# Moving the attention front's pieces to other steps inside the slots stage of a four-layer kernel

## The reference

```
# attention (channel-wise heads, 16 of 8 channels)
q, k, v = x @ qkv_w.T + qkv_b
k = layernorm(k);  v = layernorm(v)                  # over the 8 channels of a head
kv = einsum('bhqd,bhqe->bhde', k, v) / Q * temperature + attn_bias
att = einsum('bhqd,bhde->bhqe', q, kv) + x
out = gelu(att @ p1_w.T + p1_b) @ p2_w.T + p2_b + x
# ffn (soft mixture of experts, 16 experts of 64 slots)
x = layernorm(x) * g + b;  logits = einsum('bnd,esd->bnes', x, layernorm(slot_embeds) * scale)
dispatch = softmax(logits, over tokens);  combine = softmax(logits, over all slots)
slots = einsum('bnd,bnes->besd', x, dispatch)
eout = (gelu(slots @ Wg + bg) * (slots @ Wu + bu)) @ Wd + bd
out = combine @ eout
```

## Time and profile before

| | us |
|---|---|
| median of three runs | 2087.67 |
| the profiled execution's own time | 2088.02 |
| its span, first to last instruction | 2086.20 |
| TensorE busy | 1903.0 (91%) |
| VectorE busy | 1672.0 (80%) |
| ScalarE busy | 1492.8 (72%) |
| GpSimd busy | 1214.2 (58%) |
| granted TensorE clock, mean | 0.963 of full |

### The profile page before, as it was taken

How to read it: one execution, slowest core, us unless ns; L and a number is a source line. 1 busy time by engine, 2 the same in 40 slices (tenths; PEclk the granted TensorE clock), 3 DMA queues, 4 the chain that set the end, 5 groups by cost and what they waited for, 6 DMA issues and landing times.

```text
span 2086.2 us, 38852 instructions
## 1 busy us (share of the span) xinstructions
PE 1903.0 (91%) x13494; PEld 1465.1 (70%) x13494; DVE 1672.0 (80%) x3871; ACT 1492.8 (72%) x2979; POOL 1214.2 (58%) x1026
## 2 busy tenths in 40 slices
PE   4899999999999999688996999999999888889998
PEld 3677676767777676554684888888887666668797
DVE  7898999999998997376197888888888787764686
ACT  5788888888888887254376777777777677776675
POOL 3878888787978875167063555555555544437300
PEclk7999999999999999599997999999999999999999
DMA  6999898898989884201000000000001000012000
GB/s 189 335 308 324 298 319 298 312 308 305 318 302 322 297 300 167 92 1 40 1 7 1 1 1 1 1 1 1 1 1 32 1 1 1 1 38 85 11 1 41
DMA packets 72264, 263.99 MB, mean 127 GB/s; under 512 B 10822, under 2 KB 30406, under 8 KB 71558
## 3 DMA queue, kind: packets, MB, share of 16 engines
q1 hardware_dynamic: 71126, 256.53, 36.1%
q10 hardware_dynamic: 944, 4.98, 0.6%
HBM read 140.17 MB, written 121.31 MB: 125 GB/s over the span
## 4 chain that ended last, share of the span: by engine, by line
PE 42%; DVE 6%; ACT 6%; POOL 1%; issue 1%; DVEq 0%; ACTq 0%; POOLq 0%
PE PS L157 11%; PE PS L335 8%; PE PS L161 8%; PE PS L163 8%; PE PS L162 8%; ACT AR L167 3%; ACT L167 1%; DVE DR L181 1%; DVE AR L185 1%; ACT PT L171 1%; DVE PT L181 1%; POOL AR L176 1%; DVE AR L193 1%; POOL X L181 0%; DVE AR L181 0%
## 5 line engine op out<-in xcount | busy, mean ns | idle before, releaser
L167 ACT ACTIVATE AR<-PS,AR 128x512 f32<-128x512 f32 x1024 | 698.7, 690 | 204.1 <-DVE AR L193 91.3
L193 DVE TENSOR_REDUCE AR<-PS 128x1 f32<-128x512 f32 x896 | 615.4, 687 | 91.8 <-PE PS L163 76.4
L335 PE MATMUL PS<-ident,AR 128*128 128x128 f32 x3816 | 581.7, 277 | 30.6 <-DVE PT L181 16.2
L335 PEld LDWEIGHTS PS<-ident,AR 128*128 128x128 f32 x3816 | 445.2, 142 | 124.9 <-issue 44.2
L157 PE MATMUL PS<-AR 128*128 128x128 bf16 (+7 forms) x4126 | 485.7, 357 | 48.8 <-DVE AR L1379 14.1
L181 POOL TENSOR_TENSOR AR<-AR 128x512 f32<-128x512 f32 (+6 forms) x325 | 389.0, 1215 | 193.0 <-DVE AR L181 82.7
L176 POOL TENSOR_SCALAR AR<-AR 128x512 f32<-128x512 f32 (+1 forms) x146 | 255.0, 1747 | 273.5 <-DVE AR L1762 203.4
L171 ACT ACTIVATE AR<-PS 128x512 f32<-128x512 f32 (+3 forms) x596 | 348.7, 587 | 49.2 <-PE PS L157 27.0
L157 PEld LDWEIGHTS PS<-AR 128*128 128x128 bf16 (+4 forms) x4126 | 291.0, 131 | 124.7 <-issue 62.7
L171 ACT ACTIVATE PT<-PS 128x512 fp32r<-128x512 f32 x320 | 191.5, 598 | 165.6 <-PE PS L335 131.9
L181 DVE TENSOR_TENSOR AR<-PS,AR 128x512 f32<-128x512 f32 (+3 forms) x321 | 211.6, 660 | 66.9 <-PE PS L157 61.0
(11 more groups left out here) (175 smaller groups left out, 2981.6 us busy)
## 6 DMA issues: line engine op xcount, KB each, us to landing
scr<-AR SPq DMA_DIRECT2D x128, 800.0 KB, 4.3
XN<-scr SPq DMA_DIRECT2D x85, 768.0 KB, 6.7
AR<-scr SPq DMA_DIRECT2D x43, 768.0 KB, 6.6
AR<-qsc SPq DMA_DIRECT2D x96, 192.0 KB
qsc<-AR SPq DMA_DIRECT2D x16, 384.0 KB, 4.0
qsc<-AR SPq DMA_DIRECT2D x16, 256.0 KB, 4.5
AR<-in_wgu SPq DMA_DIRECT2D x16, 256.0 KB, 3.1
qsc<-AR SPq DMA_DIRECT2D x16, 128.0 KB, 4.0
```

Of the source, the lines that this page charges most:

```text
L167: return ac.e.activation(out, in_, func, bias=bias, scale=scale, accum_out=accum)
L193: return dv.e.tensor_reduce(out, in_, AX.X, ALU.max, negate=True)
L335: return pe.e.transpose(out, in_, ident[0:k, 0:k])
```

## The change

The four dictionaries get other step numbers, and hold tuples, so that one engine can do two pieces in one step; `in_order` unpacks them. In steps after `8 b`:

| piece | before | after | | piece | before | after |
|---|---|---|---|---|---|---|
| TensorE kv0 | 3 | 4 | | VectorE z | 2 | 3 |
| q | 4 | 6 | | kv0 | 4 | 5 |
| kv1 | 5 | 6 | | kv1 | 6 | 7 |
| km | 13 | 16 | | v1 | 8 | 10 |
| kq | 15 | 20 | | vn | 10 | 13 |
| ScalarE hi | 2 | 3 | | km | 14 | 17 |
| qt | 5 | 7 | | ta | 16 | 21 |
| sq | 7 | 9 | | GpSimd lo | 3 | 5 |
| root | 9 | 12 | | pb | 5 | 7 |
| xnh | 10 | 13 | | gb | 11 | 14 |
| | | | | polo | 13 | 15 |

`tr` (1), `p1` (23), `gelu` (24), `p2` (26) and `x2` (27) stay. Before, the logarithm of batch b + 2 came one step after the gelu of batch b; after, four steps after it, in the step that follows a slots copy.

```diff
-        F_PE = {1: "tr", 3: "kv0", 4: "q", 5: "kv1", 13: "km", 15: "kq", 23: "p1", 26: "p2"}
-        F_DV = {2: "z", 4: "kv0", 6: "kv1", 8: "v1", 10: "vn", 14: "km", 16: "ta", 27: "x2"}
-
-
-        F_AC = {2: "hi", 5: "qt", 7: "sq", 9: "root", 10: "xnh", 24: "gelu"}
+
+        F_PE = {1: ("tr",), 4: ("kv0",), 6: ("q", "kv1"), 16: ("km",), 20: ("kq",), 23: ("p1",), 26: ("p2",)}
+        F_DV = {3: ("z",), 5: ("kv0",), 7: ("kv1",), 10: ("v1",), 13: ("vn",), 17: ("km",), 21: ("ta",), 27: ("x2",)}
+
+        F_AC = {3: ("hi",), 7: ("qt",), 9: ("sq",), 12: ("root",), 13: ("xnh",), 24: ("gelu",)}
         AMID = ("qt", "root")
-        F_PO = {3: "lo", 5: "pb", 11: "gb", 13: "polo"}
+        F_PO = {5: ("lo",), 7: ("pb",), 14: ("gb",), 15: ("polo",)}
...
-            at = {u: [(pieces[u - 8 * b], b) for b in range(NB) if u - 8 * b in pieces] + ([(inputs[u], 0)] if u in inputs else [])
+            at = {u: [(what, b) for b in range(NB) for what in pieces.get(u - 8 * b, ())] + ([(inputs[u], 0)] if u in inputs else [])
                   for u in range(-PRE3, STEPS3)}
```

More of the change, by code:

```diff
@@ L2061, in program @@
         o_st = sem("out_st")
-        F_PE = {1: "tr", 3: "kv0", 4: "q", 5: "kv1", 13: "km", 15: "kq", 23: "p1", 26: "p2"}
-        F_DV = {2: "z", 4: "kv0", 6: "kv1", 8: "v1", 10: "vn", 14: "km", 16: "ta", 27: "x2"}
-        F_AC = {2: "hi", 5: "qt", 7: "sq", 9: "root", 10: "xnh", 24: "gelu"}
+        F_PE = {2: ("tr",), 4: ("kv0",), 6: ("q", "kv1"), 16: ("km",), 20: ("kq",), 23: ("p1",), 26: ("p2",)}
+        F_DV = {3: ("z",), 5: ("kv0",), 7: ("kv1",), 10: ("v1",), 13: ("vn",), 17: ("km",), 21: ("ta",), 27: ("x2",)}
+        F_AC = {3: ("hi",), 7: ("qt",), 9: ("sq",), 12: ("root",), 13: ("xnh",), 24: ("gelu",)}
         AMID = ("qt", "root")
-        F_PO = {3: "lo", 5: "pb", 11: "gb", 13: "polo"}
+        F_PO = {5: ("lo",), 7: ("pb",), 14: ("gb",), 15: ("polo",)}
         I_PE = {0: "st0", 2: "st1"}
```

## The result

The changed kernel takes 2093.97 us (median of 7 runs, 2091.97 to 2097.74), the kernel before on the same chip 2088.16 (7 runs): ratio 1.0027, 95% interval 1.0017 to 1.0036. Forecast was 2083.7; the change makes the kernel slower by 0.3%.

What follows compares the result with a forecast made beforehand. The slots stage was taken as bound by a chain of waits that changes engines, no engine being full. Start -7.1, five rounds +3.9, last round -1.7 and end +0.9 gave -4.0 us: 2083.7 us, range 2074 to 2094.

Steps and rivals of the forecast that it cites:

- start: Slots stage up to the slots product of step 22: reached at 1689.0 instead of 1696.06, -7.1 us.
- rounds: Five regular eight-step rounds of the slots stage: 27.1 us each instead of 26.33, together +3.9 us.
- last round: Last full round of the slots stage, without some copies, an addition and products: 23.5 against 25.29, -1.7 us.
- The end: After the last round: batch 7's key product hides, its attention product adds about 0.86; +0.9 us on 21.70.
- The change as read: The reading of the diff that the forecast used: tr stays in step 1, so no term for it.
- A new round, from V6: Chain from the start of a round's step-6 slots product to the next: 9.05 + 2.45 + 7.16 + 5.56 + 2.86 = 27.1 us.
- Table loads: ScalarE in the slots stage: four loads per round instead of three, six more, 7.7 us more work in two lumps.
- (e): In the start: steps 19 to 22 take 13.0 us, ending at 1689.0 instead of 1696.06, -7.1.
- (d): In the start: batch 0's key product at 1668.4, the transposes of step 19 at 1676.0 instead of 1683.28.
- (c): In the start: VectorE's next scaling must wait for GpSimd's affine of batch 0, which runs to 1666.9.
- the start gives nothing: Rival: the start's waits only move to the tokens of layer 2's last batch; 2090.8 us, no change; chance 0.15.
- The clock: Rival: TensorE's clock falls after idle in step 6, 2.86 becoming about 5.0; seven places, +15 us, 2099; chance 0.22.

Runs made afterwards that it cites:

- e1: The changed kernel with the token transposes (tr) back in step 1 instead of 2: 2093.69 us, ratio 1.0023 to the kernel before.
- e2: The kernel before with only the later pieces moved (root, vn, xnh, gb, polo, km, kq, ta), all earlier pieces left: 2074.30 us, ratio 0.9932.
- e7: The changed kernel with tr, hi, z, lo and kv0 back in the steps of the kernel before: 2088.10 us, ratio 1.0002.
- e9: e2 plus the query's side moved as in the change (q 6, qt 7, sq 9, v1 10), kv1 and pb not: 2082.28 us, ratio 0.9971.
- e5: The changed kernel with ScalarE's gelu replaced by a plain copy with bias: 2091.79 us, ratio 1.0016.
- e6: The changed kernel with root's logarithm and exponential replaced by plain copies: 2083.36 us, ratio 0.9973.
- e3: The changed kernel with GpSimd's affine of batch 0 cut to 8 columns instead of 1024: 2088.51 us, ratio 1.0001.
- e4: e1 with VectorE's attention sum (ta) in step 22 instead of 21: 2088.47 us, ratio 0.9997.
- e11: e2 with the second feed-forward product (p2) in 27, its sum in 28, and VectorE's z in step 3: 2067.52 us, ratio 0.9904.

## Why the prediction was wrong, step by step

The forecast was -4.0 us and the measurement in the slots stage +5.15. The 9.2 between them are: start 3.7, rounds 3.6, last round 0.65, and the 1.2 us by which the run was late already. The end is right in size. The largest step that failed is the start; with it alone put right the sum is -0.3, no change. The overlooked `tr` (2.2 in the rounds) and the one long round and the one behind it (1.7) carry it above zero. The rounds' own chain, +3.9 forecast, was 0.4 less (+3.5 with 27.03 a round).

*The change as read.* Failed. "`tr` (1) ... stay" was a misreading of the diff. e1 puts 0.43 us a round on it, about 2.2 of the 3.6, of which the start of the changed kernel has 1.4 back. It is no excuse: e1, the kernel as I had read it, took 2093.69 us.

*A new round, from V6.* The chain is the one forecast, and its size nearly. E1 at V6 + 9.05 is 9.2. E4 9.6 later is 10.15 (tr's transposes, 0.36, and the row of r3 behind them). From r4's exponential to r6, 5.56, is 5.40. r6's 2.86 is 2.69. TensorE's idle ahead of r6, "about 2 us, put down to VectorE's subtraction", is 1.93, and the idle of r2, 2.46 before, is 0.3. So 27.46 a round against 27.1 forecast and 27.03 with tr where I had it. The mechanism was right, and it was already slower than before; e2, e7 and e9 show what I had not asked: which of the moves made it so. Of the 3.0 us between e2's round and the changed kernel's, q's product in r6 is 0.85, kv1's 0.87, the addition of kv0 in r5 0.6, tr and hi between E1 and E4 0.6, and the square behind E1 0.1.

*Table loads.* Right: six more instructions, two lumps of two loads. e5 and e6 give their price: gelu's pair 0.57 us a round, the logarithm's pair 1.54. Neither pair costs its 2.56 in full.

*The start.* Failed, and this is the largest term. Steps 19 to 22 took 12.7 us, 13.0 forecast, so (e) is right; but batch 0's key product began at 1675.12 and not at 1668.4 (d), and step 19's transposes at 1681.12 and not at 1676.0, 1.2 us of each being the run's lateness. Step (c) saw GpSimd's affine block VectorE's next scaling of 512 columns, as in the earlier trace rows, and gave it one lock until 1666.9. It blocked the statistics of layer 2's last batch first, operations of four columns, through the affine and then through the next two operations of GpSimd: until 1670.3. That batch's row then kept ScalarE and TensorE waiting. The rival "the start gives nothing" named this place ("the tokens of layer 2's last batch") and was half right: 3.4 of 7.1 came. e3 confirms the cause: without the affine of batch 0 the start is 5.0 us shorter, 37.52, and the regular rounds are the same. pb in step 7 adds to the blocking: it is the last of the three blocking operations (1669.01), and in e2, with pb in 5, the third VectorE operation took its usual time:

```profile
1668.48 0.16 DVE L176 TENSOR_SCALAR AR<-AR 128x4 f32<-128x4 f32 x1
```

What that is worth at the start no run shows, since none moves pb alone: e9 has pb in 5, and its V6 of step 22 comes where the changed kernel's does (1692.7 against 1692.6). Of the 2.0 us between e2 and the changed kernel there, q's side takes as much in e9, and how it acts on the start was not tested.

*The clock.* The rival was real, and small. In the third r6 the granted clock is 0.68 over the stretch, between the levels of 1.2 and 2.4 GHz, and it takes 3.97 us instead of 2.69. That round took 28.76 and the next 27.90: 1.7 of the 139.12. Ahead of it TensorE was idle 1.92 us, as in every round, and the other rounds did not fall. Of the five profiles with an idle of 1.6 to 1.9 us in this place (the changed kernel, e1, e3, e4, e5) three have one such round, two none. "It decides from two such rounds on": there was one. By this profile the kernel is still slower than before without it.

*The last round* gave 1.05 instead of 1.7 (from 25.29 to the forecast 23.5 it is 1.8, a slip of 0.1 in the sum); which of its terms was too large was not worked out. *The end* took its 0.9.

*The range* held the time at its very edge (2093.97 of 2094), by luck: it reached that far for a clock that falls in half of the rounds, and one fell. The forecast named faster, and I had given slower 0.22.

## What to carry to other kernels

When one change moves two groups of pieces, work out each group alone, by where each instruction lands: in a gap that the bounding chain leaves, or behind it. Here one group was worth -14 us and the other +20, and a product of 0.86 us cost nothing in one step and 0.86 in the next but one. Where two waits ended at the same place, removing either gave nothing in the round and both together gave 0.9 us.

Beside GpSimd's long tensor_tensor operations look for VectorE's smallest operations, not only its large ones: here three of them lasted as long as the GpSimd operations that they met, and a layer norm's statistics are on somebody's path. Look in the trace of the kernel before for small operations that last ten times too long; there was one here. And read the step numbers from the kernel itself, not from a table made of them.

## What the runs showed of the hardware

- VectorE operations on four columns, 0.15 to 0.18 us each alone, took 1.18 and 1.23 us, and three in a row 3.70, beside GpSimd's operations with two inputs, and ended with them to 0.05 us. Two other VectorE operations beside the same affine did not: the maximum of a piece in PSUM at 1663.48 took its usual 0.68, and the reciprocal of one column at 1664.08 its 0.15.
- Logarithm, exponential, gelu and exponential cost four table loads of 1.28 us a round, and after each the next function began 0.01 to 0.02 us later.
- The granted clock over the five rounds was 0.96 before, 0.99 in the changed kernel and 1.00 in e2 and e11. In the kernel before, the stretch behind the idle of r2 had a clock of 0.56 in one round and 0.67 in the next, and behind the same idle of 2.46 us at 1734.58 it was 1.00 (1735.50 to 1739.50):

```profile
1760.66:1764.50 3.84, 3.84 (x14) 3.34 (x14) 3.68 (x8) 2.29 (x5) 1.49 (x1) 0.56 0.00 2
...
1786.50:1790.50 4.00, 3.31 (x13) 3.01 (x14) 3.16 (x7) 2.98 (x7) 0.96 (x1) 0.67 0.00 0
```

  The idle of r2 is gone in the changed kernel, and this loss with it; the kernel was slower all the same.
